# Sort stage of a two-layer graph kernel: the one-hot of destination rows stored with its 128 parts innermost

## The reference

```python
h = relu(layernorm(x))
x = x + layer0(edges, h)     # 8 heads, softmax over the edges of each src, values of dst; layernorm
h = relu(layernorm(x))
x = x + layer1(edges, h)     # cosine attention, softmax over the edges of each src
# with, in both layers, a segment_sum over src
```

## Time and profile before

| what | value |
|---|---|
| median of three executions | 5031.41 us (5024.79 to 5034.38) |
| profiled execution, own time | 5026.55 us |
| its span in the trace | 5024.8 us |
| busy in the span | DVE 80%, PE 73%, POOL 67%, PEld 60%, ACT 47% |
| mean granted clock of TensorE | 0.80 of full |
| first `is_place` of the sort to its last copy out of PSUM | 117.03 to 636.52 us |
| busy in those 519.49 us | DVE 461.69, ACT 451.90, PE 360.85, PEld 239.79, POOL 182.10 us |

### The profile page before, as it was taken

One profiled execution on the slowest core, in us unless ns is written; L12 is line 12 of the kernel. 1 busy time (PEld: TensorE's weight loads), 2 busy tenths in 40 slices (PEclk: granted clock), 3 DMA queues, 4 the chain that ended last, 5 costly groups with the idle time before them and its releaser, 6 DMA issues. The chain is left out here.

```text
span 5024.8 us, 105377 instructions
## 1 busy us (share of the span) xinstructions
PE 3675.6 (73%) x21325; PEld 3039.8 (60%) x21326; DVE 4043.6 (80%) x12191; ACT 2382.1 (47%) x8352; POOL 3368.2 (67%) x3469
## 2 busy tenths in 40 slices
PE   5676667778777777787777077777777777778776
PEld 1444445556565555565655067777777677777775
DVE  7988878888888888888888667777777777777776
ACT  3888821111111111111111656677677767776774
POOL 0333467777777777777777077777777777777773
PEclk7888867776777777767777588898888988898997
DMA  2000033333333433343333122222222222222222
GB/s 49 15 26 27 17 103 115 117 119 116 117 116 117 118 117 117 116 119 116 117 117 116 26 73 70 68 68 68 69 67 69 67 68 68 69 68 67 69 68 54
DMA packets 206181, 412.66 MB, mean 82 GB/s; under 512 B 66573, under 2 KB 97588, under 8 KB 205816
## 3 DMA queue, kind: packets, MB, share of 16 engines
q0 software_dynamic: 136384, 329.69, 24.3%
q1 hardware_dynamic: 67596, 75.74, 4.8%
q10 hardware_dynamic: 1836, 4.03, 0.3%
HBM read 363.52 MB, written 42.48 MB: 81 GB/s over the span
## 5 line engine op out<-in xcount | busy, mean ns | idle before, releaser
L912 POOL DMA_INDIRECT h_rows<-h_table,idx_ring x1652 | 1569.7, 950 | 631.4 <-issue 487.4
L912 POOL DMA_INDIRECT kv_rows<-kv_table,idx_ring x1668 | 1599.2, 959 | 514.7 <-issue 506.0
L1120 PE MATMUL psum<-vx,hot 128*128 128x136 f32 x3336 | 828.0, 389 | 409.1 <-DVE acc L1151 396.1
L1120 PEld LDWEIGHTS psum<-vx,hot 128*128 128x128 f32 x3336 | 632.5, 262 | 584.1 <-DVE acc L1151 554.7
L1073 ACT ACTIVATE vx<-clip 128x32 f32<-128x32 f32 x417 | 95.6, 229 | 1741.2 <-DVE clip L1193 1741.2
L1612 DVE SCALAR_TENSOR_TENSOR h_sb<-h_sb,corr,psum 128x129 f32 x1668 | 582.7, 349 | 419.3 <-PE psum L1570 176.6
L1109 PE MATMUL psum<-q_sb,hotT 128*128 x3336 | 682.0, 368 | 68.8 <-DVE prod L1166 53.6
L1109 PEld LDWEIGHTS psum<-q_sb,hotT 128*128 128x128 f32 x3336 | 580.0, 262 | 204.2 <-issue 204.0
L1560 PE MATMUL psum<-ident,hotl 128*128 128x128 f32 x1668 | 308.6, 315 | 470.7 <-DVE highs L1638 469.2
L1151 DVE TENSOR_TENSOR acc<-acc,psum 128x136 f32 x1668 | 489.2, 293 | 162.9 <-issue 38.6
L1617 DVE SCALAR_TENSOR_TENSOR prod<-psum,h_rows 128x128 f32<-128x128 f32 x1668 | 511.2, 345 | 78.8 <-DMA h_rows<-h_table,idx_ring 73.0
(11 more groups left out here) (225 smaller groups left out, 5366.2 us busy)
## 6 DMA issues: line engine op xcount, KB each, us to landing
hand<-h_table SPq DMA_DIRECT2D x2048, 0.5 KB
kv_rows<-kv_table,idx_ring POOLq DMA_INDIRECT x1668
own_rows<-own SPq DMA_DIRECT2D x104, 256.0 KB, 2.6
own<-own_rows SPq DMA_DIRECT2D x104, 256.0 KB
h_rows<-h_table,idx_ring POOLq DMA_INDIRECT x1652
kv_table<-kv SPq DMA_DIRECT2D x21, 256.0 KB, 2.2
out<-q_sb SPq DMA_DIRECT2D x2, 1536.0 KB
h_sb<-h_now SPq DMA_DIRECT2D x21, 128.0 KB, 2.0
```

The costliest lines, as they stand in the source:

```text
L912: pool.indirect_dma_start(out=G[:, k, j, :], out_offset=None, in_=table, in_offset=bass.IndirectOffsetOnAxis(ap=idx[:, k, j:j + 1], axis=0 ...
L1120: last = nc.tensor.matmul(S_ps[j // HALF][:, j % HALF, :], hot[:, k, j * P:(j + 1) * P], vx[:, k, j, :], start=True, stop=True)
```

## The change: the element order of `to_part`

```diff
@@ the tile
-        to_part = part_room.bitcast(bf16)[:, 0:BRING * P * BATCH].rearrange("p (k n c) -> p k n c", k=BRING, c=BATCH)
+        to_part = part_room.bitcast(bf16)[:, 0:BRING * P * BATCH].rearrange("p (k c n) -> p k c n", k=BRING, c=BATCH)
@@ PE, the ten products of a batch
                     for c in range(BATCH):
-                        last = nc.tensor.matmul(place_ps[r], to_part[:, k, :, c], pieces[:, k, c, :],
+                        last = nc.tensor.matmul(place_ps[r], to_part[:, k, c, :], pieces[:, k, c, :],
                                                 start=(b == 0 and c == 0), stop=(b == BATCHES - 1 and c == BATCH - 1))
@@ DVE, the one-hot of the parts
-                    tt(to_part[:, k, :, :], under(part_of[:, r, col:col + BATCH], P),
-                       place_no[:, :, :], ALU.is_equal).then_inc(s_topart, 1)
+                    tt(to_part[:, k, :, :], over(part_of[:, r, col:col + BATCH], P),
+                       place_no[:, :, :].rearrange("p n c -> p c n"), ALU.is_equal).then_inc(s_topart, 1)
```

## The result

The changed kernel takes 5244.55 us in the median (5238.78 to 5250.61, 4 runs), against 5032.32 us (5024.79 to 5034.38) for the kernel before: a ratio of 1.0421, 95% interval 1.0408 to 1.0434. It is slower by 4.2%, some 212 us. The forecast was 5242, within 5085 to 5300.

A forecast was written before the change was run, and what follows sets the result against it. The prediction took DVE to set the sort's pace in 17 of 18 chunks; +14.5 us in chunk 0, +191.8 in chunks 1 to 16 and +5 in the last made +211, so 5242 us, within 5085 to 5300.

The forecast's parts named there:

- The bound: In the sort, DVE has the most work in 17 of 18 chunks, with 3.1 us of slack a chunk.
- PE's side is worth nothing: L534's gapless weights load 41 ns faster each, but PE waits for ACT longer, so nothing counted; 10.7 us at most.
- The sign that I gave for it: L534's weight loads on PE would show near 97 ns, as the gapless load of L476 does.
- The price of L798: On DVE, L798 loses pairs and pays for gaps in `place_no`: 2.43 us each, 1.61 more than before.
- one price for each access to a new place: Reason for L798's price: ACT's gapped read and DVE's gapped write both cost nearly 1.8 ns an element.
- The sum: Over the sort: chunk 0 +14.5, chunks 1 to 16 +191.8, chunk 17 +5, together +211 us.
- the middle term: Chunks 1 to 16: DVE's work 644.6 us plus 9.0 idle, less 461.9, so +191.8 us.
- the wait for POOL in batch 3: L798 waits there for POOL's L424 to end; claimed already counted in DVE's 412.2 us and unchanged.
- The gaps are free: Rival: L798 falls only to the single rate, 1.48 us; whole +61, 5093 us; chance 0.10.
- In between: Rival: L798 takes 1.84 us, by L713's small price for gaps; whole 5150 us; chance 0.10.
- a factor: Rival: gaps multiply DVE's rate as ACT's, L798 at 2.23 ns an element, 3.00 us; whole +302, 5333 us; chance 0.10.
- Not slower: Rival: L798 keeps pairs at 0.82 us and gapless weights shorten PE, up to 10.7 us less, 5021 us; chance 0.05.

The follow-up runs named there:

- row_table: The changed kernel, with L798 reading a gapless row of the 128 numbers in place of `place_no`: 5081.24 us, ratio 1.0107 to the kernel before.
- part_f32: The kernel before, with only `part_of` kept in f32 instead of bf16: 5081.99 us, ratio 1.0107 to the kernel before.
- pairs: The changed kernel, with `to_part` laid out with two columns side by side and a table holding every number twice: 5024.51 us, ratio 0.9996 to before.
- place_pairs: The kernel before, with only `is_place` laid out in pairs of columns and `to_part` as it was: 4950.88 us, ratio 0.9848.
- pairs_both: Both `to_part` and `is_place` laid out in pairs of columns, measured against the kernel before: 4957.43 us, ratio 0.9852.
- steps: The changed kernel, with L798 reading number tables at steps of 1 to 16 elements, differing by batch: 5171.93 us in one run.
- write_curve: The changed layout with gapless inputs, `to_part` written in orders differing by batch, and one added instruction in three batches: 5429.19 us in one run.

## Why the prediction was right

- *The bound.* DVE sets the pace in 17 of 18 chunks, and its idle 3.1 us a chunk is all that can soak up new work. Right: in chunks 1 to 16 its idle time went from 49.6 to 2.9 us. I kept 9.0, the slack of chunk 0.
- *PE's side is worth nothing.* Right, and shown three times, each within the scatter: `row_table` against `part_f32`, `pairs` against before, `place_pairs` against `pairs_both`. The sign that I gave for it failed: the loads did not show 97 ns in the changed kernel but 146 in the median. In chunks 1 to 16 PE is busy 384.43 of 650.37 us where it was 325.19 of 461.86, and the granted clock there is 0.74 where it was 0.88; the gapless load of L476, which the change does not touch, went from 97 to 144 ns in the same way. In `row_table`, at 98, the forecast price holds.
- *The price of L798.* 2.43 us forecast, 2.46 measured. Both parts stand alone: pairs lost 0.66 us (`row_table`, 1.48), gaps 0.98 us (`steps`). The mechanism, pairs lost and then a price for the gaps, is right; that its size came out so close is luck. The row that I took it from was a write, L796, and no run shows that a read of two bytes must cost what a write of four does: taken from a write of bf16 it would have been 4.45 ns and 5.8 us. My reason, one price for each access to a new place, does not hold: reads at 4 and 8 bytes pay nothing, and writes pay by their width. ACT's read at the same step gives 1.80 ns by the earlier trace rows, but only if its whole price is carried over; its extra of 0.96 ns on DVE's 1.039 would be 2.00 ns, its factor 2.23.
- *The sum.* Chunk 0 +13.8 (14.5 forecast), chunks 1 to 16 +188.5 (191.8), the last +4.9 (5): +207 for 211. The two errors in the middle term, 2.9 us too little in DVE's work (235.3 for 232.4) and 6.1 too much idle, half cancel. L798 alone, from 134.5 to 377.0 us in these chunks, grew by 10.1 us more than forecast; DVE's busy time outside L798 shrank by 7.3. Some 6.5 of the 10.1 are a step of the prediction that failed, though the total hardly shows it: that the wait for POOL in batch 3 "stays". There L798 went from 1.86 us in the mean of chunks 1 to 16 to 3.91, so its excess over an undisturbed L798 grew from 1.04 to 1.45 us: L424 started 0.5 to 1.1 us ahead of L798 and now starts 0.3 to 0.4 us ahead.
- *The rivals.* "The gaps are free" is exactly `row_table`: 54 us for 61. "In between" (1.84 us) and "a factor" (3.00 us) fell with L798's 2.46 (the first has +108 in its sum where its terms give +107, which changes nothing). "Not slower" needed pairs in an order that has none; `pairs` gave it the pairs, and the gain was still not there.
- *Not foreseen.* The last scatters end later. From the last chunk's end to the first instruction of the next stage on POOL it is 16.0 us (843.69 to 859.73), where before it was 9.7 (636.52 to 646.18): 6 us more. When the chunk ends, one indirect DMA of POOL is still under way (834.07 to 846.31); why it takes 12.24 us is open. The rest of the 224 us between the two profiled executions, some 10 us, lies behind the sort; the one after is the slowest of its four, and the medians differ by 212. So it is also luck that the total of +211 is met to 1 us: the sort brought 4 us less than forecast, and the scatters 6 us that I had not counted.

## What to carry to other kernels

A layout change has two sides, and each engine's instruction is to be costed on its own side: a weight load that gets 40 ns shorter on an engine that waits is worth nothing, an instruction that triples on the engine that sets the pace costs its increase less the idle time that it fills (the 162 L798 grew by 272 us together, the sort by 207). For 16-bit tensors on VectorE first ask whether all operands still step by one element, then how far apart the accesses are; rows of two elements keep the pairs and bring a reader's step from 20 down to 4 bytes. And look at who reads the neighbouring tile: there the same layout brought 1.5%.

## What the runs showed of the hardware that was not expected

- Single-rate reads of 1,280 bf16 elements on DVE paid nothing for gaps up to 8 bytes a step (1.47 to 1.48 us), 1.56 us in all at 10 and 2.45 to 2.49 from 16 to 32 bytes (`steps`, with the other input at a step of zero). The Trainium skill (Vector Engine (DVE) Microarchitecture Reference, 5.2 Measured stream behaviour on trn2) asks for runs of two neighbouring 4-byte words at full rate, measured on 4-byte elements; a step of 8 bytes has no neighbours and was still at full rate here, so the measurement decides.
- A DVE write of two bytes took 4.45 ns an element at steps of 20, 256 and 384 bytes, one of four bytes 1.72 at 256 (`write_curve`).
- Where DVE's two-input instructions and POOL's product overlap, one of the two engines loses time, and not always the same one. In chunks 1 to 16 of the changed kernel POOL's product L424 takes 1.95 us and DVE's L798 beside it 3.91 in the mean, in place of 2.46. In chunk 0 and in the last chunk L424 takes 7.68 and 7.57 us. The three cases, from the timelines of the two engines (chunk 0, a middle chunk, the last):

```profile
129.94 7.68 POOL L424 TENSOR_TENSOR ends<-is_place,pk_now 128x960 f32<-128x960 bf16 x1 [102.04 <-DVE is_place L789]
...
414.46 1.95 POOL L424 TENSOR_TENSOR ends<-is_place,pk_now 128x960 f32<-128x960 bf16 x1 [23.79 <-DVE is_place L789]
414.80 3.91 DVE L798 TENSOR_TENSOR part_room<-part_of,place_no 128x1280 bf16<-128x1280 bf16 x1
...
818.32 2.46 DVE L798 TENSOR_TENSOR part_room<-part_of,place_no 128x1280 bf16<-128x1280 bf16 x1
818.50 7.57 POOL L424 TENSOR_TENSOR ends<-is_place,pk_now 128x960 f32<-128x960 bf16 x1 [15.16 <-DVE is_place L789]
...
820.67 0.67 DVE L789 TENSOR_TENSOR is_place<-place_b,place_no 128x960 bf16<-128x960 bf16 x1
821.24 2.46 DVE L798 TENSOR_TENSOR part_room<-part_of,place_no 128x1280 bf16<-128x1280 bf16 x1
...
823.60 0.67 DVE L789 TENSOR_TENSOR is_place<-place_b,place_no 128x960 bf16<-128x960 bf16 x1
824.30 3.43 DVE L796 TENSOR_TENSOR ends<-is_place,pk_now 128x960 f32<-128x960 bf16 x1
```

In the last chunk POOL ends at 826.07, after four DVE instructions with two inputs and within a fifth that itself takes 3.43 us in place of 1.8. The same L424 took 2.47 us before, with L798 at 0.82, and 3.13 in `row_table`, with L798 at 1.48. The Trainium skill (SBUF — State Buffer, Who interferes with whom) has a DVE instruction with two inputs in SBUF and a GpSimd instruction that reads SBUF contend for one port; the timeline agrees, and no run here took the contention away by itself.
